# Flamingo layer on one core: the last batch's sums, GpSimd's column steps, the first stage's order and warm-up changed

## The reference

```python
def _aft_local(emb, wq, bq, wk, bk, wv, bv, wo, bo, pos_bias):
    q = emb @ wq + bq
    k = emb @ wk + bk
    v = emb @ wv + bv
    mask = (jnp.abs(idx[:, None] - idx[None, :]) < S)      # S = 64, T = 512
    w = pos_bias * mask
    ek = jnp.exp(k - jnp.max(k, axis=1, keepdims=True))
    ew = jnp.exp(w - jnp.max(w, axis=1, keepdims=True))
    num = jnp.einsum('tj,bjd->btd', ew, ek * v)
    den = jnp.einsum('tj,bjd->btd', ew, ek)
    y = jax.nn.sigmoid(q) * num / den
    return y @ wo + bo

emb = x + pos_encod                                  # x is layer-normalised, pos_encod is ctx
a = _layer_norm(attn + emb, gamma, beta)
ff = jax.nn.relu(a @ w1 + b1) @ w2 + b2              # 256 -> 1024 -> 256
xattn = _layer_norm(ff + a, gamma, beta)

def _bitlinear(x, w):                                # int8-like tokens, weights -1, 0, 1
    return jnp.einsum('bsi,oi->bso', _act_quant(x), _weight_quant(w))

x = x + tanh(g_xattn) * xattn
gate = silu(_bitlinear(ln(x), w_gate)); up = _bitlinear(ln(x), w_up)
out = x + tanh(g_ffn) * _bitlinear(gate * up, w_down)
```

## Time and profile before

| | us |
|---|---|
| median of 3 runs | 513.0 |
| the profiled execution's own time | 510.02 |
| its span, first to last instruction | 508.3 |
| TensorE matmuls busy | 480.5 |
| VectorE busy | 438.0 |
| ScalarE busy | 375.5 |
| GpSimd busy | 248.8 |

### The profile page before, as it was taken

The page is one execution under the profiler, slowest core; times in us unless marked ns, Lnnn a source line. Parts: engine busy times, 40 slices in busy tenths (PEclk is TensorE's granted clock), DMA queues, the critical chain, the costliest instruction groups (busy, mean ns, idle before and its releaser), DMA issues.

```text
span 508.3 us, 9743 instructions
## 1 busy us (share of the span) xinstructions
PE 480.5 (95%) x3010; PEld 397.2 (78%) x3010; DVE 438.0 (86%) x1002; ACT 375.5 (74%) x611; POOL 248.8 (49%) x389
## 2 busy tenths in 40 slices
PE   6898999999999999999999999999999999999483
PEld 6687888988877887788977987788878987887242
DVE  6889989786989899898989899898899888959574
ACT  3474869957778788696868688687769687899673
POOL 7292364169234493248535484248325902664511
PEclk9797999999999999999999999999999999999688
DMA  5963242232202331222312330223124201243301
GB/s 186 186 209 125 43 166 84 41 43 85 62 1 45 81 105 44 42 63 74 94 23 45 102 89 17 43 63 80 47 42 63 75 10 23 63 95 44 93 0 43
DMA packets 69330, 36.03 MB, mean 71 GB/s; under 512 B 47008, under 2 KB 68768, under 8 KB 69280
## 3 DMA queue, kind: packets, MB, share of 16 engines
q1 hardware_dynamic: 68448, 35.41, 27.7%
q10 hardware_dynamic: 832, 0.00, 0.1%
HBM read 20.46 MB, written 4.19 MB: 48 GB/s over the span
## 4 chain that ended last, share of the span: by engine, by line
PE 83%; DVE 6%; issue 3%; DMA 3%; ACT 2%; POOL 1%; SPq 0%; DVEq 0%; POOLq 0%
PE ps L2501 60%; PE ps L2658 8%; PE ps L2680 4%; PE ps L2567 3%; PE ps L2509 2%; PE ps L2518 2%; DVE cols L1737 2%; DMA work<-in_L_xattn_wo_dram 2%; DMA w_bit<-place_c 1%; PE ps L2575 1%; PE ps L2593 1%; DVE work L1731 1%; DVE ps L1657 1%; PE ps L2535 1%; DVE st L1595 1%
## 5 line engine op out<-in xcount | busy, mean ns | idle before, releaser
L554 POOL TENSOR_TENSOR mv<-mv,cols 128x2 f32<-128x2 f32 x64 | 13.2, 206 | 168.0 <-DVE mv L1603 167.8
L2501 PE MATMUL ps<-w_hi,h_hi 128*128 128x256 f32 x256 | 75.8, 296 | 0.0
L2501 PE MATMUL ps<-w_lo,h_hi 128*128 128x256 f32 x256 | 71.5, 279 | 0.0
L2501 PE MATMUL ps<-w_hi,h_lo 128*128 128x256 f32 x256 | 71.4, 279 | 0.0
L2501 PE MATMUL ps<-n1T_hi,w_hi 128*128 128x512 f32 (+1 forms) x144 | 54.1, 376 | 0.4 <-DVE n1T_lo L1686 0.3
L1657 DVE RECIPROCAL ps<-ps 128x512 f32<-128x512 f32 x16 | 53.7, 3358 | 0.2 <-PE ps L2575 0.2
L931 ACT ACTIVATE h_hi<-ps,cols 128x512 fp32r<-128x512 f32 (+1 forms) x72 | 45.4, 637 | 11.3 <-PE ps L2501 10.1
L2501 PE MATMUL ps<-n1T_lo,w_hi 128*128 128x512 f32 (+1 forms) x144 | 53.3, 370 | 0.0
L2501 PE MATMUL ps<-n1T_hi,w_lo 128*128 128x512 f32 (+1 forms) x144 | 53.2, 370 | 0.0
L2501 PEld LDWEIGHTS ps<-w_hi,h_hi 128*128 128x128 f32 x256 | 48.2, 188 | 3.0 <-DVE h_lo L1692 0.3
L977 ACT ACTIVATE work<-ps,cols 128x1024 f32<-128x1024 f32 x32 | 35.7, 1114 | 19.8 <-DVE work L1731 10.0
(11 more groups left out here) (179 smaller groups left out, 1481.5 us busy)
## 6 DMA issues: line engine op xcount, KB each, us to landing
x_in<-in_x_dram SPq DMA_DIRECT2D x16, 256.0 KB, 2.9
emb<-in_ctx_dram SPq DMA_DIRECT2D x16, 256.0 KB, 2.9
work<-in_x_dram SPq DMA_DIRECT2D x8, 512.0 KB, 4.1
out_dram<-work SPq DMA_DIRECT2D x16, 256.0 KB, 2.2
work<-in_L_xattn_w_dram SPq DMA_DIRECT2D x2, 1024.0 KB, 8.9
work<-in_L_ffn_w_gate_dram SPq DMA_DIRECT2D x1, 1024.0 KB, 5.7
work<-in_L_ffn_w_up_dram SPq DMA_DIRECT2D x1, 1024.0 KB, 5.8
place_c<-in_L_ffn_w_down_dram SPq DMA_DIRECT2D x1, 1024.0 KB, 8.9
```

The source lines that it names most:

```text
L2501: last = nc.tensor.matmul(dst, lhsT, rhs, start=(i == 0 and not begun), stop=(i == n - 1 and ends))
```

## The change

It has several parts.

- Two of the column steps of each product (hfac and hout) go from VectorE's `product_scale` to a new GpSimd step `product_factors`, for all 8 batches and 4 tiles.
- In the last batch x1 is the tile x_in, and n3 with its half-precision view is the tile emb. `first_sum` of that batch no longer waits for outputs of batch 6; the output of the last batch waits for the store before it.
- SyncE loads both halves of batch 0's tokens first and then ctx; wk and wv before wq and wo; w1 before w2; some later loads stand in another place.
- VectorE embeds batch 0 in GpSimd's place. The memset of far_sel goes behind two other steps of VectorE.
- 88 idle transposes in place of 50.
- All engines' lists and the table of banks are written out anew: `beta_w1` and far_weights stand earlier, TensorE's last feed of batch 7 stands ahead of the last gates of batch 6, and many steps change places by a few.

```diff
--- before.py
+++ after.py
 
-WARM_UP = 50
+WARM_UP = 88
...
 BANK = {
-    ("embT", 0): (0, 7, 6, 5, 0, 4, 0, 4), ("embT", 1): (1, 3, 7, 0, 7, 6, 7, 6), ("kT", 0): (2, 1, 1, 5, 3, 3, 3, 0),
...
+    ("embT", 0): (0, 7, 2, 6, 3, 1, 2, 0), ("embT", 1): (1, 0, 4, 2, 7, 5, 7, 3), ("kT", 0): (2, 2, 5, 3, 3, 2, 2, 5),
...
-EWT_BANKS = (1, 6, 7, 1)
-TOTAL_BANKS = (7, 6, 4)
-B1_BANK, FAR_BANK = 7, 5
+EWT_BANKS = (3, 6, 7, 5)
+TOTAL_BANKS = (5, 1, 3)
+B1_BANK, FAR_BANK = 7, 3
...
-        xn, n1, n2, n3 = x_in, res, a2, out_t
+        xn, n1, n2 = x_in, res, a2
+
+
+        def sum_of(b):
+            return x_in if b == NB - 1 else x1
+
+        def n3_of(b):
+            return emb if b == NB - 1 else out_t
+
...
-        xq_h = low_half(piece(4)).rearrange("p (t d) -> p t d", t=NT)
+        def xq_h_of(b):
+            whole = emb[:].rearrange("p t d -> p (t d)") if b == NB - 1 else piece(4)
+            return low_half(whole).rearrange("p (t d) -> p t d", t=NT)
...
             fetch_x(0, 0)
+            fetch_x(0, 1)
             fetch_ctx(0, 0)
-            fetch_x(0, 1)
             fetch_ctx(0, 1)
+            fetch_wkv()
             fetch_wqo()
-            fetch_wkv()
             fetch_bias()
             fetch_x(1, 0)
             fetch_positions(0)
             fetch_vectors()
             fetch_x(1, 1)
             fetch_x_again(0)
+            fetch_w1()
             fetch_w2()
-            fetch_w1()
             fetch_ctx(1, 0)
             fetch_ctx(1, 1)
...
             store(5, 1)
+            fetch_x_again(7)
             xq_rows(6, 0)
-            fetch_x_again(7)
             xq_rows(6, 1)
...
                 wait(pool, n2g_ok, b, p + 1)
                 wait(pool, xb_ok, b, 1)
-                wait(pool, out_ok, b, 2 * p - 2)
-                pool.tensor_tensor(half(x1, p), half(n2, p), half(xb, p), ALU.add).then_inc(x1_ok.sem, 1)
+                if b == NB - 1:
+                    wait(pool, emb_ok, b, 2)
+                else:
+                    wait(pool, out_ok, b, 2 * p - 2)
...
+            def product_factors(b, t):
+
+                wait(pool, hc_hr_ok, b, 2 * t + 2)
+                wait(pool, hr_act if t % 2 else hr_pool, b, t // 2 - 1)
+                pool.tensor_scalar(hfac[:, t:t + 1], hr[:, t:t + 1], sup[:, t:t + 1], QMAX,
+                                   ALU.mult, ALU.mult).then_inc(hfac_ok.sem, 1)
+                pool.wait_ge(wdg_ok, 1)
+                wait(pool, out_ok, b, t - 3)
+                pool.tensor_scalar(hout[:, t:t + 1], hc[:, t:t + 1], wdg, None, ALU.mult).then_inc(hout_ok.sem, 1)
 
...
             rsqrt(0, 0, 0)
             rsqrt(0, 0, 1)
-            embed(0, 0)
-            embed(0, 1)
             rsqrt(1, 0, 0)
             rows()
             add_bo(0)
             rsqrt(1, 0, 1)
             w2_lower(0)
             embed(1, 0)
+            embed(1, 1)
             w2_lower(1)
-            embed(1, 1)
             rsqrt(2, 0, 0)
             rsqrt(2, 0, 1)
...
             add_b2(7)
             x_beta(7)
+            rsqrt(7, 2, 0)
+            product_factors(6, 0)
             quantise(6, 0)
-            rsqrt(7, 2, 0)
-            quantise(6, 2)
             n2_gamma(7, 0)
             first_sum(7, 0)
+            product_factors(6, 1)
+            rsqrt(7, 3, 0)
             rsqrt(7, 2, 1)
-            rsqrt(7, 3, 0)
+            product_factors(6, 2)
+            quantise(6, 2)
             n2_gamma(7, 1)
             first_sum(7, 1)
+            product_factors(6, 3)
             rsqrt(7, 3, 1)
+            product_factors(7, 0)
             quantise(7, 0)
+            product_factors(7, 1)
+            product_factors(7, 2)
             quantise(7, 2)
+            product_factors(7, 3)
...
-                dst, src = {0: (xn, x_in), 2: (n2, a2), 3: (n3, x1)}[n]
+                dst, src = {0: (xn, x_in), 2: (n2, a2), 3: (n3_of(b), sum_of(b))}[n]
                 wait(act, nmr_ok[n], b, p + 1)
-                if n == 3:
+                if n == 3 and b == NB - 1:
+                    wait(act, embT_ps, b, 2)
+                    wait(act, embo_ok, b, 1)
+                elif n == 3:
                     wait(act, out_stored[p], b, 0)
...
             gates_and_bias()
             normalise(0, 0, 0)
-            wq_upper()
+            wkv_upper()
             normalise(0, 0, 1)
             wo_upper()
-            wkv_upper()
+            wq_upper()
             emb_upper(0, 0)
             emb_upper(0, 1)
             half_sigmoid(0, 0)
             half_sigmoid(0, 1)
             exp_positions(0)
+            exp_positions(1)
             ewT_upper(0)
-            exp_positions(1)
...
                 wait(dve, hm_ok, b, t + 1)
+                wait(dve, hout_ok, b, t - 3)
                 wait(dve, sup_ok, b, t // 2 + 1)
                 nc.vector.tensor_scalar(hc[:, t:t + 1], hm[:, t:t + 1], sup[:, t:t + 1], 1e-5,
                                         ALU.mult, ALU.max).then_inc(hc_hr_ok.sem, 1)
                 wait(dve, hc_hr_ok, b, 2 * t + 1)
                 nc.vector.reciprocal(hr[:, t:t + 1], hc[:, t:t + 1]).then_inc(hc_hr_ok.sem, 1)
-                wait(dve, hc_hr_ok, b, 2 * t + 2)
-                nc.vector.tensor_scalar(hfac[:, t:t + 1], hr[:, t:t + 1], QMAX, sup[:, t:t + 1],
-                                        ALU.mult, ALU.mult).then_inc(hfac_ok.sem, 1)
-                wait(dve, out_ok, b, 0)
-                nc.vector.tensor_scalar(hout[:, t:t + 1], hc[:, t:t + 1], wdg, None, ALU.mult).then_inc(hout_ok.sem, 1)
 
             def output(b, t):
 
                 wait(dve, d_ps, b, t + 1)
                 wait(dve, hout_ok, b, t + 1)
-                nc.vector.scalar_tensor_tensor(out_t[:, t, :], bank(b, "down", t)[:, 0:D], hout[:, t:t + 1], x1[:, t, :],
+                if b == NB - 1:
+                    wait(dve, out_stored[t // 2], b, 0)
+                nc.vector.scalar_tensor_tensor(out_t[:, t, :], bank(b, "down", t)[:, 0:D], hout[:, t:t + 1], sum_of(b)[:, t, :],
                                                ALU.mult, ALU.add).then_inc(out_ok.sem, 1)
+
+
+            def far_table():
+                dve.wait_ge(const_ok, 5)
+                nc.vector.memset(far_sel[:], 1.0).then_inc(far_rows_ok, 1)
...
+            def embed(b, p):
+                wait(dve, norm_ok[0], b, p + 1)
+                wait(dve, ctx_loaded[p], b, 16)
+                nc.vector.tensor_tensor(half(emb, p), half(xn, p), half(emb, p), ALU.add).then_inc(emb_ok.sem, 1)
...
+            far_table()
             tile_stats(0, 0, 0)
             tile_stats(0, 0, 1)
+            tile_stats(0, 0, 2)
             mean_variance(0, 0, 0)
-            tile_stats(0, 0, 2)
             tile_stats(0, 0, 3)
             mean_variance(0, 0, 1)
+            embed(0, 0)
+            wkv_lower()
+            embed(0, 1)
+            wo_lower()
             wq_lower()
-            wo_lower()
-            wkv_lower()
             emb_lower(0, 0)
             emb_lower(0, 1)
...
             weighted(0, 1)
-            add_bias(0, 2)
+            e_lower(0, 0)
+            far_weights()
+            e_lower(0, 1)
             add_bias(0, 3)
-            e_lower(0, 0)
-            e_lower(0, 1)
+            weighted(0, 2)
+            ewT_lower(1)
+            ewT_lower(2)
+            ewT_lower(3)
+            e_lower(0, 2)
+            weighted(0, 3)
             tile_stats(1, 0, 2)
...
             attend(0, "num", 0, 0)
             attend(0, "num", 0, 1)
-            attend(0, "den", 1, 1)
-            attend(0, "num", 1, 1)
             attend(0, "den", 0, 0)
             attend(0, "den", 0, 1)
+            attend(0, "den", 1, 1)
             attend(0, "den", 0, 2)
+            attend(0, "den", 1, 2)
+            attend(0, "num", 0, 2)
+            beta_w1()
+            key_sums(0)
+            attend(0, "num", 0, 3)
+            attend(0, "den", 0, 3)
+            attend(0, "den", 1, 3)
+            attend(0, "num", 1, 1)
             attend(0, "num", 1, 2)
-            key_sums(0)
-            attend(0, "num", 0, 2)
-            attend(0, "den", 0, 3)
             attend(0, "num", 1, 3)
-            attend(0, "num", 0, 3)
-            attend(0, "den", 1, 2)
-            attend(0, "den", 1, 3)
             attend_far(0, "num", 0)
             attend_far(0, "den", 0)
             attend_far(0, "den", 1)
             attend_far(0, "num", 1)
-            beta_w1()
             emb_rows(1, 0)
             emb_rows(1, 1)
...
             feed_pair(7, 7, 0)
             feed_pair(7, 0, 1)
+            hidden(7, 6, 1, HALF[1])
             gate(6, 0)
             up(6, 0)
             feed_pair(7, 1, 1)
-            gate(6, 1)
             feed_pair(7, 2, 1)
             feed_pair(7, 3, 1)
+            gate(6, 1)
             up(6, 1)
-            hidden(7, 5, 1, HALF[1])
-            hidden(7, 6, 1, HALF[1])
+            feed_pair(7, 4, 1)
+            feed_pair(7, 5, 1)
             hidden(7, 7, 1, HALF[1])
-            feed_pair(7, 4, 1)
```

(13 more changed lines are left out.)

1485 lines of the change are left out of this document (752 added, 733 removed), and 22 rows, old and new, of the table BANK.

## The result

The changed kernel takes 516.6 us (median of 6; 514.91 to 519.54), the kernel before 512.65 (6; 511.32 to 513.44): ratio 1.009, 95% interval 1.0065 to 1.0114, 4 us slower. Forecast were 506.5 us and a range of 500.5 to 511.5.

What follows compares the result with a forecast made beforehand. TensorE was taken as the bound, busy 95% of the span and at full clock from 70 to 454 us, with time to gain at both ends. Head +0.3, middle -0.8, tail -6.0: -6.5, from 513.0 to 506.5 us; range 500.5 to 511.5.

Steps and rivals of the forecast that it cites:

- the head: Start through batch 1's entry: TensorE 0.3 us behind at batch 1's attention, bounds 3.0 ahead and 3.8 behind.
- the middle: Between the two ends: VectorE's relief gains 0.8 us of TensorE's 1.2 us idle time, bounds -1.2 and +2.
- the tail: Batch 7 to the end: no waits for batch 6's outputs and an earlier last feed give -6.0 us, bounds -3 and -9.
- Start: To batch 0's queries: clock stays up, idle before first real transpose 0.5 us, queries from 17.0, done 2.2 us earlier.
- 31.8 us for the second group of attends: Batch 0's attention: far-weight instructions now precede e_lo and the second ew_lo, which VectorE's new order reaches at 31.8 us.
- All of batch 0's attention with them is done at 42.7: Head: with one-column matmuls in front of key_sums, batch 0's attention ends at 42.7 us against 43.1.
- rival 2: Batch 0's attention: one-column matmuls ahead of key_sums drop the clock, up to 3.5 us more in the head: 510.0; chance 0.16.
- GpSimd's steps: Column steps of every product: 64 at 0.20 us, 13 us on a half-idle GpSimd, covered by TensorE.
- First_sum doesn't wait: Tail: batch 7's sum in x_in waits for no batch 6 output; second sum at 475.2 instead of 482.4, 7.2 us gained.
- with today's durations: Tail: steps counted in the new order at existing durations put product(7, 0) at 481.0 against 487.21, 6.2 us earlier.
- The last feed: Tail: TensorE's last feed of batch 7 comes 4.1 us earlier, 465.4 instead of 469.5.
- Rival 3: Tail: output(6, 3) holds VectorE before product_scale(7, 0), losing the tail's gain and adding 2 us: 515.0; chance 0.10.

Runs made afterwards that it cites:

- b_warm_only: Kernel before with 88 idle transposes at the start in place of 50, nothing else changed: ratio 0.9968 to the kernel before.
- a_beta_late: Changed kernel with beta_w1 (the one-column matmuls) back behind batch 0's last far matmuls and b1_whole behind divided(0, 0): ratio 1.006 to the kernel before.
- a_far_late: Changed kernel with far_weights late again, their PSUM bank apart from the first denominators', and ewT_lower(1) earlier: ratio 1.003 to the kernel before.
- b_factors: Kernel before with only hfac and hout of every product on GpSimd, in front of the quantisation that needs them: ratio 1.0471 to the kernel before.
- b_start: Kernel before with the change's 88 idle transposes, first loads, weights' order, batch 0 embedding on VectorE and far table: ratio 0.9982 to the kernel before.
- a_both_late: Changed kernel with both head moves undone, far weights late and beta_w1 behind the attention: ratio 0.9994 to the kernel before.
- a_down_early: a_tail_idle with down(5, 1) in front of hidden(7, 0), as in the kernel before: ratio 0.9967 to the kernel before.
- a_dve_factors: a_both_late with hfac and hout back on VectorE and GpSimd's steps for them taken out: ratio 1.0038 to the kernel before.
- b_homes: Kernel before with only the last batch's x1 in x_in and n3 in emb, no list changed: ratio 0.9997 to the kernel before.
- a_tail_idle: a_both_late with output(6, 3) behind product_scale(7, 0), and idle transposes before down(6, 1), xq_rows(7, 0) and down(6, 2): ratio 0.9964 to the kernel before.

## Why the prediction was wrong, point by point

By the traces, each of the three terms failed: the head was to cost 0.3 us and cost 5.9 (lag at 69 us), the middle was to give 0.8 and cost 4.5, the tail was to give 6.0 and gave about 1. The medians say 4 us slower where these terms add up to 9.5, so each of them can be too large by part of the difference. The head is the one that experiments settle: undoing its two moves brings the ratio from 1.009 to 0.9994.

- **Start: right.** Clock 1.00, queries from 17.27 (17.0 forecast), wo_lo 0.69 us without GpSimd's embedding beside it (1.34 before). The idle time before the first real transposes was 1.67, not 0.5 (the 88 took 11.14 us here and 12.58 in b_warm_only), and did no harm: the clock stayed up. That 88 alone brings all of it I had not seen.
  The Trainium skill, "SBUF — State Buffer", section "Who interferes with whom", says that a VectorE instruction with two inputs in SBUF and one of GpSimd that reads SBUF exclude each other. By that rule wo_lo runs at its own speed here, and the trace agrees (0.69 against 1.34 us).
- **The far weights.** "31.8 us for the second group of attends" held (31.70). What failed is the step that treated this as a delay of one group: the attention stood still three times (1.26, 0.30 and 0.83 us beyond the usual distance between the starts of two attends, from 28.3 on), and the clock fell behind it, at 31.7 us. a_beta_late has these waits and the fall, a_far_late neither. I had also overlooked that far_bank and the first denominators share PSUM bank 3, so that TensorE waits for far_w itself. With a_far_late: 0.6%.
- **The clock with beta_w1 inside: the failed step.** "All of batch 0's attention with them is done at 42.7" measured 47.4. The sum took full clock for the whole attention and put its fall at nothing there; it stood only in the bounds and in rival 2. Half clock from 31.7 to 35.0 and from 40.0 to 45.2 us costs about 1.6 and 2.6 us (half of these stretches), and the one-column matmuls took 0.7 more than before, as the second stretch began over them, with 0.62 of the clock from 38 to 40 us: 4.9 us, which is the miss. From the attention's end to batch 1's queries it then took 5.9 us, as forecast (42.7 to 48.7); the 3.6 us of the one-column matmuls on the path were priced. What was not priced is what follows the wait that they no longer cover: TensorE waited 3.17 and 0.98 us, and the stretch at half rate of batch 1's entry then lay on the queries, to 59.0 us (before, to 50.5), by the lag some 2 us more. That the one-column matmuls had been free is true of the kernel before: there they ran beside the reciprocal, within the 9.4 us from the last far matmul to those queries. With them back there: 0.3%.
- **Rival 2** had the mechanism (clock falls inside the attention) at 510.0 and "up to 3.5 us". In the changed kernel the fall cost 4.9, since the waits behind the far weights, which the rival does not name, brought a stretch of their own. a_far_late shows the rival's part alone: one stretch of 3.4 us. The rival's time missed as well, as it kept the forecast's tail and middle.
- **Middle.** Forecast -0.8, bounds -1.2 and +2. The lag grew by 4.5 us between 69 and 454 us, by 1.9 to 5.8 in the other kernels with the new lists, and by 0.4 to 1.4 in those with the old (b_factors apart, with 24). The waits of the changed kernel, and of the kernel before, between 70 and 454 us:

```profile
PE ps L2747 <- DMA w_bit<-place_c: 2.6, 3, 1.7
PE ps L2568 <- DVE n1T_lo L1743: 1.2, 1, 1.2
PE ps L2568 <- DVE y_lo L1731: 0.8, 2, 0.4
```

```profile
PE ps L2680 <- DMA w_bit<-place_c: 0.5, 1, 0.5
PE ps L2501 <- DVE n1T_lo L1686: 0.3, 1, 0.3
```

  The bound of +2 was too narrow. In this trace the 2.6 us are TensorE reaching down before the column is there; but b_start and b_warm_only, with the old lists, have 1.8 and 1.9 us of such waits too, and a_both_late, with the new ones, has none. A wait of 1.1 to 1.7 us for n1T_lo is in every trace with the new lists but that of a_down_early, which only exchanged it for another. That it is the lists and not GpSimd's hop is suggested by a_dve_factors, where the lag still grew by 4.0; which of their steps, no run has shown.
- **GpSimd's steps** took 0.26 and 0.29 us instead of 0.20: 17.8 us busy for 64; no wait of TensorE between 70 and 454 us names them directly. Whether the relief of VectorE is worth the forecast 0.8 us is not shown: in the old lists no run tests it in a good place, and the 0.4% of a_dve_factors holds for the new lists only.
- **Tail.** Forecast -6.0 with bounds -3 and -9; measured about -1. "First_sum doesn't wait" and its 7.2 us held to 4.6 us. The step that failed is the count from there on "with today's durations": the gates of batch 7 stood behind down(6, 2), which waited for its column, and ran at half clock, and product(7, 0) waited 1.72 us for them. From product(7, 0) to the last reciprocal it then took 14.3 us instead of the 13.0 forecast: the wait of 1.71 us and the work for output(6, 3) were not paid by the four shorter products. The last feed, forecast 4.1 us earlier, came 2.3 earlier (477.5 less 10.4, against 469.4): TensorE waited 1.67 us for its h_lo, which VectorE makes behind product(6, 1) and its scale. b_homes (0.9997, within 0.2% of no change) shows that the wait named in the earlier trace rows was not what bound the end.
- **Rival 3** (output(6, 3) holds VectorE) was there with 1.71 us, not enough to be slower by itself.

Why the trace of before is 2.6 us faster than its median is open in part. Among the 30 recorded executions of the kernel before on one chip, the 12 with a mean granted clock of 0.969 and more took 509.97 to 512.11 us, the 10 with 0.963 and less 511.95 to 514.18. The trace has 0.969, that of b_homes 0.959, and 1.1 of the 3.0 us between these two lie in the first 22 us, where both kernels do the same. Where the rest lies stays open.

## What to carry to other kernels

Work that fills a wait is free only where it stands: before moving it, write down what that wait is without it, and at which clock the work behind it will run. Where a wait of TensorE names one releaser, look for the second that is nearly as late (here the DMA'd column, the clock, the output in front) before booking the wait as a gain; undoing one part at a time, with nothing else touched, is the cheap test. And check whether a step that you move frees a buffer for a load.

## What the runs showed of the hardware that I had not expected

- Idle transposes of the identity keep the granted clock at 1.00 over the 15 us of the tail that hold TensorE's waits (0.98, 0.50 and 0.83 became 1.00 each, from 475 to 490 us). Placed where the clock is already down they run at half rate and delay what follows (18 in 3.85 instead of 2.18 us).
- The 32 one-column matmuls took 3.63 us at full clock and 5.63 in a_both_late, where the clock was at its lower level for most of them, though each writes only one column. In a_far_late the clock fell 1.1 us behind them, with TensorE busy without a break from 32 to 40 us.
- The moment at which the warm-up reaches its full rate differs between executions: the 88 idle transposes took 11.14 us in the changed kernel, 11.44 in b_start and 12.58 in b_warm_only, with 21 of them between 5 and 7 us in the first and 11 in the last.
- The same lists, started at another time, differ by 2 to 4 us in the middle (lag growth 1.9 in a_both_late, 5.3 in a_tail_idle, whose lists are equal there but for output(6, 3) and the idle transposes, both behind 454 us). Waits of 1 to 2 us for a column transposed by DMA are in one of these traces and not in the other.
